# The router's factors of an expert stage, spread over the partitions by DMA instead of by products with a selection matrix

## What is computed

```python
logits = (flat @ router_w).astype(jnp.float32) + router_bias
probs = jax.nn.softmax(logits, axis=-1)
top_w, top_i = jax.lax.top_k(probs, TOPK)                # 2 of 16
norm_w = top_w / (jnp.sum(top_w, axis=-1, keepdims=True) + 1e-06)
combine = jnp.sum(jax.nn.one_hot(top_i, E, dtype=norm_w.dtype) * norm_w[..., None], axis=1)
routed = combine[:, E - 1:E] * flat
for e in range(E - 1):
    y = jax.nn.silu(flat @ expert_gate_w[e]) * (flat @ expert_up_w[e]) @ expert_down_w[e]
    routed = routed + combine[:, e:e + 1] * y
...
shared = jax.nn.silu(gate) * (hidden_states @ shared_up_w) @ shared_down_w
return shared + routed
```

## Time and profile before

| | us |
|---|---|
| time, median of 3 runs | 1104.1 |
| lowest and highest | 1103.48, 1104.55 |
| the profiled execution | 1103.15 |
| its span in the profile | 1100.9 |

### The profile page before, as it was taken

The page is one execution under the profiler, slowest core; times in us unless marked ns, Lnnn a source line. Parts: engine busy times, 40 slices in busy tenths (PEclk is TensorE's granted clock), DMA queues, the critical chain, the costliest instruction groups (busy, mean ns, idle before and its releaser), DMA issues.

```text
span 1100.9 us, 22207 instructions
## 1 busy us (share of the span) xinstructions
PE 1086.2 (99%) x8911; PEld 692.0 (63%) x8911; DVE 813.0 (74%) x1247; ACT 592.0 (54%) x939; POOL 796.3 (72%) x524
## 2 busy tenths in 40 slices
PE   9999999999999999999999999999999999999998
PEld 7898998877755545555555555455555545457886
DVE  4658766476676887887887888878878887896553
ACT  5634453476666555555555555555555655644442
POOL 5879998644467899898798799899899898950000
PEclk9999999999999999999999999999999999999999
DMA  8322332200000002000000000000000000000000
GB/s 267 116 80 96 118 98 97 80 1 1 1 1 1 1 1 106 2 1 1 1 1 1 1 1 1 1 1 1 1 1 1 1 1 1 1 1 10 10 1 19
DMA packets 25621, 31.04 MB, mean 28 GB/s; under 512 B 2080, under 2 KB 21920, under 8 KB 24240
## 3 DMA queue, kind: packets, MB, share of 16 engines
q1 hardware_dynamic: 25200, 29.62, 8.0%
q10 hardware_dynamic: 320, 0.01, 0.0%
HBM read 20.19 MB, written 9.44 MB: 27 GB/s over the span
## 4 chain that ended last, share of the span: by engine, by line
PE 87%; DVE 6%; POOL 2%; issue 2%; ACT 2%; DVEq 0%; POOLq 0%; ACTq 0%
PE o_ps L1722 19%; PE mx_ps L1676 7%; PE st_ps L1706 5%; PE st_ps L1700 5%; PE st_ps L1703 5%; PE ha_banks L651 4%; PE bank L2135 3%; PE bank L2137 3%; PE bank L2136 3%; PE mx_ps L1609 3%; PE pj_ps L1628 2%; PE pj_ps L1620 2%; PE ha_banks L704 2%; PE ha_banks L715 2%; PE st_ps L1697 1%
## 5 line engine op out<-in xcount | busy, mean ns | idle before, releaser
L2049 POOL TENSOR_TENSOR acc<-acc,prob 128x1024 f32<-128x1024 f32 x192 | 468.8, 2442 | 61.8 <-ACT prob L1870 51.6
L1870 ACT ACTIVATE prob<-st_ps 128x1024 f32<-128x1024 f32 x256 | 248.5, 1022 | 206.3 <-PE st_ps L1706 206.2
L1722 PE MATMUL o_ps<-prob,v_cur 128*64 128x512 f32 x1024 | 245.6, 599 | 0.0
L1941 DVE TENSOR_REDUCE mx_part<-mx_ps 128x1 f32<-128x512 f32 x258 | 164.9, 667 | 72.1 <-PE mx_ps L1676 72.1
L1722 PEld LDWEIGHTS o_ps<-prob,v_cur 128*64 128x64 f32 x1024 | 68.0, 136 | 96.3 <-issue 78.2
L1944 DVE TENSOR_REDUCE mx_part<-mx_ps 128x2 f32<-128x1024 f32 x78 | 93.6, 1200 | 44.1 <-PE mx_ps L1676 44.1
L1960 DVE RECIPROCAL rden<-rden 128x128 f32<-128x128 f32 x128 | 120.6, 943 | 0.0
L1676 PEld LDWEIGHTS mx_ps<-k_hi,q_hi 64*128 64x128 f32 x414 | 46.5, 183 | 107.0 <-issue 94.6
L1676 PE MATMUL mx_ps<-k_hi,q_hi 64*128 64x512 f32 x414 | 111.6, 456 | 1.5 <-DVE mx_part L1944 0.8
L1706 PE MATMUL st_ps<-q_hi,d_lo 64*128 64x512 f32 x512 | 100.6, 389 | 0.0
L2049 POOL TENSOR_TENSOR acc<-prob 128x1024 f32<-128x1024 f32 x32 | 76.1, 2379 | 26.0 <-PE pj_ps L1605 18.9
(11 more groups left out here) (419 smaller groups left out, 2302.5 us busy)
## 6 DMA issues: line engine op xcount, KB each, us to landing
v_rows<-ha_v SPq DMA_DIRECT2D x8, 1024.0 KB, 4.0
ha_vt<-v_rows SPq DMA_DIRECT2D x16, 512.0 KB, 4.0
h_w<-in_h SPq DMA_DIRECT2D x2, 1024.0 KB, 7.9
w_raw<-in_w SPq DMA_DIRECT2D x8, 192.0 KB, 3.7
head_wkv<-in_wkv SPq DMA_DIRECT2D x2, 512.0 KB, 4.7
m_w<-in_m SPq DMA_DIRECT2D x3, 256.0 KB, 3.0
out<-fin SPq DMA_DIRECT2D x3, 256.0 KB, 2.2
sel_raw<-in_sel SPq DMA_DIRECT2D x1, 576.0 KB, 8.5
```

The source lines that it names most:

```text
L1722: mm = pe.matmul(o_ps[rows(h), :], v_cur[:, m % 2, j, rows(h)], prob[:, (16 * m + slot) % RING, h, :], start=(j == 0), stop=(j == KT - 1), ...
L1870: act.activation(prob[:, n % RING, :, :], st_ps[:, slot % 2, :, :], ACT.Exp, scale=SCALE).then_inc(s_exp, 1)
L1941: dve.reduce_max(mx_part[:, h, i, keys:keys + 1], maxima_banks(q, n)[h], AX_X).then_inc(s_mxr, 1)
L2049: pool.tensor_tensor(total, old, new, ALU.add).then_inc(s_acc, 1)
```

## The change

- `cm` takes the factors unrounded, in one VectorE product (`cw` and the low part are gone); the ones stay in column 16.
- SP stores rows 0 to 31 of `weights_t` to DRAM, one store for each chunk (`sync_store`).
- For each pair and chunk, and once more for `own`, SP loads a tile of 128 x 512: two DMAs, each of which reads one row of DRAM for 64 partitions (`sync_load`). That makes 36 tiles, in five places in turn: two where `sel` was, three in places of the second attention's tokens of chunk 3, which are free until then. At most two tiles are under way; a tile is loaded anew when the step five items before has used it.
- `h` and `own` read such a tile in place of `w_ps`. The 36 products with `sel` are gone, and `sel` with its load and its rounding on GpSimd.
- The loads of `w_raw` go between the tile loads in four pairs. `diag_all` and `wo` come after the last tile.
- The second attention's first maxima wait for another semaphore, since their banks are no longer `w_ps`. VectorE's last `xr` waits for the last `h` and `own`.

```diff
@@ first_norm
-            dve.tensor_tensor(cw[:, :, :], wt[:, :, :], wide(rtwo), ALU.mult).then_inc(s_route, 1)
+            dve.wait_ge(s_fill, 3)
+            dve.tensor_tensor(cm[:, :, E], wt[:, :, :], wide(rtwo), ALU.mult).then_inc(s_route, 1)
...
-        elif i == LOGITS + 7 and place == 0:
...
-            dve.tensor_copy(cm[:, :, E].bitcast(F32R), cw[:, :, :]).then_inc(s_route, 1)
-            dve.wait_ge(s_route, ROUTE["hi"])
-            dve.tensor_tensor(cm[:, :, LO:LO + EXPERTS].bitcast(F32R), cw[:, :, :], cm[:, :, E], ALU.subtract)\
-               .then_inc(s_route, 1)
...
-        pool.tensor_copy(part(sel, j), part(sel_raw, j))
@@ experts
+    def load_done(engine, i):
+        engine.wait_ge(s_wload[i % 2], 32 * (i // 2 + 1))
+
+    def sync_store(sp, k):
+        sp.wait_ge(f.s_wt, k + 1)
+        sp.dma_start(w_rows[k], weights_t[0:LO, k, :]).then_inc(s_wstore, 16)
+
+    def sync_load(sp, i):
+
+        k, e = i // EACH, i % EACH
+        if e == 0:
+            sp.wait_ge(s_wstore, 16 * CHUNKS if k >= 2 else 32)
+        if i >= 2:
+            load_done(sp, i - 2)
+        if i == 2:
+
+            sp.wait_ge(head.s_vo, head.VALUES)
+        if i >= TILES:
+            k_was, e_was = (i - TILES) // EACH, (i - TILES) % EACH
+            if e_was < EPAIRS:
+                sp.wait_ge(s_h, k_was * EPAIRS + e_was + 1)
+            else:
+                sp.wait_ge(s_own, k_was + 1)
+        upper, lower = (2 * e, 2 * e + 1) if e < EPAIRS - 1 else (2 * e, EXPERTS) if e < EPAIRS else (EXPERTS - 1, EXPERTS - 1)
+        for half, row in enumerate((upper, lower)):
+            sp.dma_start(w_tile(i)[half * HD:half * HD + HD, :], w_rows[k][row:row + 1, :].to_broadcast([HD, CH]))\
+              .then_inc(s_wload[i % 2], 16)
...
-        pe.matmul(w_ps[n % 2], sel[:, tile(e)], weights_t[:, k, :], start=True, stop=True).then_inc(s_w, 1)
...
-            pe.matmul(w_ps[0], sel[:, EPAIRS * P:], weights_t[:, k, :], start=True, stop=True).then_inc(s_w8, 1)
...
-        dve.wait_ge(s_w, n + 1)
+        load_done(dve, item(n))
         dve.wait_ge(s_su, n + 1)
-        dve.tensor_tensor(h[n % RING][:, :], su[n % 2][:, :], w_ps[n % 2], ALU.mult).then_inc(s_h, 1)
+        dve.tensor_tensor(h[n % RING][:, :], su[n % 2][:, :], w_tile(item(n)), ALU.mult).then_inc(s_h, 1)
...
-            dve.wait_ge(s_w8, k + 1)
-            dve.tensor_tensor(own[:, :], xn[:, k, now], w_ps[0], ALU.mult).then_inc(s_own, 1)
+            load_done(dve, k * EACH + EPAIRS)
+            dve.tensor_tensor(own[:, :], xn[:, k, now], w_tile(k * EACH + EPAIRS), ALU.mult).then_inc(s_own, 1)
@@ two_layers
+        LOADS = range(e.TILES + 1, e.TILES + 5)
...
-                head.sync(sp)
+                for n in range(TURNS):
+                    if n % 2 == 0:
+                        head.sync_values(sp, n // 2)
+                    head.sync_turn(sp, n)
+                    if n == TURNS - 3:
+                        e.sync_store(sp, 0)
+                        e.sync_store(sp, 1)
+                    if n == TURNS - 2:
+                        e.sync_load(sp, 0)
+                        e.sync_load(sp, 1)
+                e.sync_store(sp, 2)
+                e.sync_store(sp, 3)
+                for i in range(2, e.ITEMS):
+                    e.sync_load(sp, i)
+                    if i in LOADS:
+                        t2.sync_weights(sp, LOADS.index(i))
                 t2.sync(sp)
```

More of the change, by code:

```diff
@@ L1034, in head_attention, with experts @@
     return s
-def experts(nc, c, f, head, x, xn, xr, xr_hi, xr_lo, eps, weights_t, moe_w, sel, at, only, keep):
+def experts(nc, c, f, head, x, xn, xr, xr_hi, xr_lo, eps, weights_t, moe_w, w_rows, w_tiles, at, only, keep):
     s = Const()
-    banks = at.banks(*((n, [P, CH]) for n in ("g_ps0", "u_ps0", "g_ps1", "u_ps1", "w_ps0", "w_ps1", "y_ps", "n_ps")))
-    g_ps, u_ps, w_ps = ([banks[i][:, :] for i in of] for of in ((0, 2), (1, 3), (4, 5)))
+    banks = at.banks(*((n, [P, CH]) for n in ("g_ps0", "u_ps0", "g_ps1", "u_ps1", "free0", "free1", "y_ps", "n_ps")))
+    g_ps, u_ps = ([banks[i][:, :] for i in of] for of in ((0, 2), (1, 3)))
     y_ps, n_ps = (t[:, :] for t in banks[6:])
@@ L1079, in norms, with item, w_tile @@
         return n // EPAIRS - 1, NORMS[slice(*NORMS_AT[n % EPAIRS])] if n % EPAIRS else ()
+    EACH, TILES = EPAIRS + 1, len(w_tiles)
+    ITEMS = CHUNKS * EACH
+    def item(n):
+        return n // EPAIRS * EACH + n % EPAIRS
+    def w_tile(i):
+        return w_tiles[i % TILES][:, :]
+    def load_done(engine, i):
[21 more added lines that the diff above has]
+              .then_inc(s_wload[i % 2], 16)
     def parts(n):
@@ L1533, in chunk, with sync_weights @@
         return q // PAIRS * HALVES + half
+    def sync_weights(sp, n):
+        if n == 0:
+            sp.wait_ge(head.s_yc, head.TURNS)
+        for p in (2 * n, 2 * n + 1):
+            sp.dma_start(w_raw[:, p, :], a["w1"][p, :, :]).then_inc(s_w, 16)
     def sync(sp):
-        sp.wait_ge(head.s_yc, head.TURNS)
-        for p in range(PAIRS):
-            sp.dma_start(w_raw[:, p, :], a["w1"][p, :, :]).then_inc(s_w, 16)
         sp.wait_ge(s_fill, 1)
@@ L2378, in two_layers @@
             moe_raw[n] = Region(nc, start).sb(f"{n}_raw", [P, size])
-        start = room.at
-        sel = room.sb("sel", [CW, (EPAIRS + 1) * P], F32R)
-        sel_raw = Region(nc, start).sb("sel_raw", [CW, (EPAIRS + 1) * P])
+        w_tiles = [room.sb(f"w_tile{i}", [P, CH]) for i in range(2)]
+        w_tiles += [Region(nc, XR + 8 * KB * i + 6 * KB).sb(f"w_tile{2 + i}", [P, CH]) for i in range(3)]
+        w_rows = nc.dram_tensor("w_rows", (CHUNKS, LO, CH), F32, kind="Internal").ap()
         HEAD = room.at
@@ L2394, in two_layers @@
         late = Region(nc, FIRST)
-        e = experts(nc, c, first, head, x, xn, xr, xr_hi, xr_lo, eps, weights_t, moe_w, sel, at, only, keep)
+        e = experts(nc, c, first, head, x, xn, xr, xr_hi, xr_lo, eps, weights_t, moe_w, w_rows, w_tiles, at, only, keep)
         t2 = second_attention(nc, c, head, e, a, xr, xr_hi, xr_lo, early, pairs, late, at)
```

86 lines of the change are left out of this document (33 added, 53 removed).

## The result

| | before | after |
|---|---|---|
| median, lowest, highest (4 runs each) | 1104.21, 1103.48, 1104.55 | 1116.12, 1115.70, 1117.11 |
| the profiled execution, its span | 1103.15, 1100.9 | 1115.70, 1113.8 |

The ratio is 1.0111, 95% interval 1.0095 to 1.0127. The forecast was 1113, range 1098 to 1119.

The account below looks back on a forecast made before the run. TensorE looked full, but VectorE's full stretch and the norm's chain also set the time. Blocking there 9.4, first chunk +0.6, end +0.3, head -0.25: about +10 us on 1103.15 or 1104.1, so 1113, range 1098 to 1119.

Parts of the forecast that it names:

- The blocking, and that it costs more than the products give: Experts stage: VectorE with two SBUF inputs and GpSimd block each other; net slower by about 10 us, 64% for +4 to +14.
- A stretch from the last `su` to `n1cen`: From a chunk's last step to the next norm's mean, VectorE is full; blocking costs 2.2 us in each of three passes.
- the replay: Fourth chunk's start: successive `h` and `own` lose 0.9, 0.05, 0.7, 0.7 us, the fifth free; 2.35 in sum, less 0.15 for overlap.
- The chain behind the mean: Single dependences from the norm's mean to the second variance: a blocked `h` delays `xn` and `r1sq`, 0.94 us per pass.
- First chunk: Plain steps only: blocked step 2.76 us, against 2.31 now and 2.08 if TensorE sets it; between -0.9 and +1.8, taken as +0.6.
- Head: At the end of the head, one product leaves the path: -0.25 us.
- The casts: nothing: Eight GpSimd casts for the selection matrix go; GpSimd only waits longer for ScalarE: nothing, at most 0.1 us each without that cover.
- End: End of the experts stage: one `h` is lost, mostly inside an idle time of VectorE; +0.3 us.
- Loads and `w_raw`: SP's queue: tile loads at 1.85 us each and the moved `w_raw` loads stay hidden; no cost.
- The upper end of the gain: 36 removed products at 0.23 us each: 8.3 us if TensorE's pace were the limit in every step.
- the rival of 1097 us: VectorE gets in first in most steps, GpSimd waits instead, and TensorE's pace wins; about 1097 us, chance 15%.
- What would show it: Profile signs: `h` mean 1.1 to 1.3 us, up to 1.9; longer subtractions; `n1cen` 27 to 29 us apart; TensorE idle.

Follow-up runs that it names:

- e4: Changed kernel, but from the third step on `su` is written to free PSUM banks, so `h` has one SBUF input, `own` still two; 1103.0 us.
- e7: Changed kernel with `su` in PSUM only at expert steps 4, 5, 6, so `h` keeps two SBUF inputs in the others; 1111.8 us.
- e8: Changed kernel with `su` in PSUM except at expert steps 4, 5, 6 and the first two steps, where `h` has two SBUF inputs; 1107.2 us.
- e11: Changed kernel with a GpSimd cast of 128 x 64 put back in each of the eight turns where one for `sel` was removed; 1116.4 us.
- e3: Changed kernel with wrong factors read from PSUM, no stores or tile loads, and the `w_raw` loads in one block again; 1102.1 us.
- e2: Changed kernel, but `h` and `own` read wrong factors from two free PSUM banks; stores and tile loads still run; 1104.5 us.
- e1: Changed kernel with 36 matmuls of the removed size put back, into banks that nobody reads; 1117.3 us.
- e5: e4 with `y_ps` taken three steps after its `u_ps` in place of two, a chunk's last two pairs together; 1104.9 us.
- e6: Kernel before the change with `y_ps` taken three steps late in place of two, a chunk's last two pairs together; 1105.7 us.
- e9: e4 with `own` computed by GpSimd instead of VectorE; 1104.7 us.
- e10: e9 with the two `xr_lo` of chunks 0 and 1 also moved from VectorE to GpSimd; 1102.8 us.
- e12: Kernel before the change with the two `xr_lo` of chunks 0 and 1 moved from VectorE to GpSimd; 1103.3 us.

## Why the prediction was right

**The blocking, and that it costs more than the products give: right, and shown** (e4, e7, e8). In most meetings whoever starts first makes the other wait, and the two engines, each in its own order, meet again in the next step: 20 of the 32 `h` take over 0.9 us.

**A stretch from the last `su` to `n1cen`: 2.2 us predicted, 2.9, 3.7 and 2.3 measured.** The last pass is the one that I replayed, and its sum came out (2.45 less 0.2), with `own` in the place of the first `h`. In e11, whose last A is 13.2 us, the first `h` did come behind the subtraction (275.94), and the replay holds term by term: 0.88, 0.02, 0.68 and 0.69 lost where 0.9, 0.05, 0.7 and 0.7 were predicted.

```profile
276.21 1.57 DVE L1336 TENSOR_TENSOR h<-su,w_tile 128x512 f32<-128x512 f32 x1
```

I used this pass for all three, and that is the mis-sized term. The first two passes carry the `w_lo` splits, which also have two SBUF inputs: one of them lost 0.79 (226.74) and one 0.84 us (248.02). I had named them and not priced them. The fifth `h`, which I called free, lost 0.3 in each of those two passes. The second pass had the clock's dip besides.

**The chain behind the mean: 0.94 predicted, 0.8 to 0.9 measured**, in the changed kernel and in the first two passes of e8 alike.

**First chunk: +0.6 predicted, +0.3 measured**, and between e4 and the changed kernel 0.9. But the other bound of that term was wrong: unblocked, TensorE doesn't set a step at 2.08; the two-step chain holds it at 2.10 to 2.32.

**Head: -0.25 predicted, +0.3 measured.** "The casts: nothing" was wrong if the reading above is right: that GpSimd gets earlier is no saving when it then stands in VectorE's way. **End: +0.3 predicted, 0.6 measured.** **Loads and `w_raw`: hidden, right.** A load landed in 3.0 us at the median where 2.8 was estimated; issuing took 0.60, not 0.46; the one wait was 0.5. All the terms: 10 predicted in the sum, 12.6 without the difference at the start.

**The upper end of the gain, and the rival of 1097 us.** I gave "TensorE's pace wins" 15%. e3, which has no blocked `h`, no tile loads and no products for the factors, took 1102.1: that time was out of reach. Reading as a TensorE that is busy for all of 25.50 us was the error behind it. A busy time without gaps did not mean that a matmul fewer is time won: in A VectorE was level with it, in B the chain set the time, and in the plain steps the lag did. The reading of B was not tried by itself.

**What would show it**: `h`'s mean is 1.16 (1.1 to 1.3 expected), its maximum 1.74 (1.9), subtractions reach 1.78, `own` was long once. The distances between `n1cen` are 30.0 and 28.5, the first above my 27 to 29. Not foreseen: TensorE's longest waits are for `res`, 5.6 us in three cases, as `res` stands behind the blocked products on VectorE.

## What to carry to other kernels

When an operand of a VectorE instruction is moved from PSUM to SBUF, list the GpSimd work that reads SBUF at that time before counting any saving; if the result of the step ahead can be written to a PSUM bank that has become free, that takes the price away. Test a "full" engine by taking one instruction from it: here VectorE's list, TensorE's list and the chain between them lay so close together that relieving one alone won nothing that could be told. Before you read a microsecond between two variants as the worth of an edit, look at the operations that the edit did not touch: an unchanged `w_lo` took 0.42, 1.12 or 1.49 us, depending on where it fell beside GpSimd's subtraction, and between e3 and e2 that was a shift of 0.12 us. For the same reason an edit that only makes an engine off the critical path earlier may not be free.

## What the runs showed of the hardware that I had not expected

**TensorE's clock fell for some 3 us after it had stood idle.** In the experts stage of the traces this is seen in the changed kernel, e1, e3, e5, e7, e8 and e11, and not in the kernel before, e2, e4, e6, e9, e10 and e12. Five of these seven have many blocked `h`; e3 and e5 have not. The changed kernel, in the second pass; length, PE busy, the other engines, granted clock in the third column from the right:

```profile
252.00:254.00 2.00, 0.00 (x0) 0.00 (x0) 1.97 (x3) 0.53 (x1) 0.83 (x1) 1.00 0.36 131
...
256.00:258.00 2.00, 2.00 (x6) 1.51 (x6) 1.97 (x4) 1.64 (x3) 0.65 (x1) 0.50 0.21 57
```

```profile
286.00:289.00 3.00, 2.01 (x8) 1.01 (x6) 2.87 (x4) 0.99 (x3) 1.28 (x1) 1.00 0.12 35
...
290.50:293.50 3.00, 3.00 (x8) 2.42 (x9) 0.35 (x2) 0.91 (x3) 0.75 (x1) 0.50 0.00 0
```

The second pair is e8, where TensorE was idle for a third of a stretch of 3 us shortly ahead of the fall. 0.50 is 1.2 GHz; e8's matmuls of that stretch follow each other at 0.43 us instead of 0.23. In e8 the fall met the nine `g_ps` matmuls that ScalarE waits for, and B took 16.6 us instead of 15.0. In the changed kernel it cost less: `n1cen` waited 0.4 us for the mean, and the `su` after it 0.8 for `u_ps`.

The runs of one kernel differ by it. Medians of those with a mean clock of 0.999 or 1.000 and of those below: e10 1102.57 (6 runs) and 1104.61 (5), e4 1102.93 (8) and 1105.05 (2), e8 1106.17 (2) and 1108.52 (2). The kernel before was at 0.999 or more in 70 of 73 runs beside the experiments, the changed kernel below it in all four. So something like 1 to 2 of its 12 us are the clock's, an estimate from the waits of 0.4 and 0.8 us above and from the 2 us between the groups of e4, e8 and e10. (In e5 the two runs at the higher clock are only 0.5 us faster.) At full clock e10 would be 1.4 us ahead of the kernel before (1102.57 to 1103.94); its other runs take that back. Why the same kernel falls in one run and not in the next stays open.

**At leads of a few hundredths of a microsecond the start times in the trace don't tell who will wait.** `h` at 275.49 went ahead of a subtraction that started at 275.51, and was not slowed; `xm_lo` in e11, 0.03 us ahead, was. The side that waits resumes a little before the other's row ends: `own` at 276.09, which takes 0.68 alone, ended at 277.85, so it began its work at about 277.17, 0.12 us before the subtraction's end.
